# Local attention: the value projection and the output projection exchanged on TensorE, two reciprocal-root operations behind each mask operation

## The reference, cut to what matters

```
h = shift_token(x)
q, k, v = split(h @ wqkv, 3)                    # 8 heads of 64
q = q / max(norm(q), 1e-12) * qs                # the same for k, over each head
q, k = rotary_xpos(q, k)
sim = 8 * q @ k.T   over this window and the one before (128 + 128 keys)
attn = softmax(where(mask, -max, sim))
o = attn @ v
x = x + o @ wo
```

## Time and profile before

| | us |
|---|---|
| median of 3 runs | 2124.27 |
| lowest, highest | 2120.65, 2127.5 |
| the profiled execution, its own time | 2122.05 |
| its span, first to last instruction | 2120.3 |
| PE busy | 1900.5 (90%) |
| DVE busy | 1589.2 (75%) |
| ACT busy | 1098.0 (52%) |
| POOL busy | 449.2 (21%) |

### The profile page before, as it was taken

How to read it: one execution, slowest core, us unless ns; L and a number is a source line. 1 busy time by engine, 2 the same in 40 slices (tenths; PEclk the granted TensorE clock), 3 DMA queues, 4 the chain that set the end, 5 groups by cost and what they waited for, 6 DMA issues and landing times. The chain is left out here.

```text
span 2120.3 us, 41246 instructions
## 1 busy us (share of the span) xinstructions
PE 1900.5 (90%) x13304; PEld 1640.6 (77%) x13304; DVE 1589.2 (75%) x4668; ACT 1098.0 (52%) x2551; POOL 449.2 (21%) x270
## 2 busy tenths in 40 slices
PE   4678999899999759999999689995999999959998
PEld 4657888878889748888888578884888888858887
DVE  3367776776766668999999477775899999957777
ACT  2243343342342248888888434433777777743433
POOL 1130000000000024444444100002444444410110
PEclk7889999999999979999999799997999999989999
DMA  5410000000000020000000100001000000000002
GB/s 186 172 26 1 1 1 1 1 1 1 1 1 1 13 95 6 5 5 5 5 5 5 50 20 11 10 5 66 6 5 5 5 5 5 5 20 11 11 10 84
DMA packets 46083, 46.26 MB, mean 22 GB/s; under 512 B 8660, under 2 KB 40106, under 8 KB 45992
## 3 DMA queue, kind: packets, MB, share of 16 engines
q1 hardware_dynamic: 45992, 45.07, 6.4%
HBM read 36.67 MB, written 8.39 MB: 21 GB/s over the span
## 5 line engine op out<-in xcount | busy, mean ns | idle before, releaser
L993 ACT ACTIVATE l_probs<-l_probs,l_negmax 128x256 f32<-128x256 f32 x512 | 253.2, 496 | 64.7 <-DVE l_negmax L1074 64.7
L116 PE MATMUL ps<-local_w_hi,l_xT 128*128 128x512 f32 x384 | 166.9, 435 | 37.9 <-DVE l_xT L1067 31.9
L947 POOL TENSOR_TENSOR l_t<-l_t,l_t 128x1024 f32<-128x1024 f32 x64 | 152.8, 2388 | 195.8 <-DVE l_t L1120 195.8
L951 POOL TENSOR_TENSOR l_t<-l_t,l_rnorm 128x1024 f32<-128x1024 f32 x64 | 121.9, 1905 | 307.5 <-DVE l_rnorm L1091 307.5
L999 ACT ACTIVATE l_probsT<-ps 128x512 f32<-128x512 f32 x256 | 138.5, 594 | 53.4 <-PE ps L1218 53.4
L426 ACT ACTIVATE attn_exp<-ps 128x512 f32<-128x512 f32 x128 | 76.5, 599 | 152.1 <-PE ps L118 151.9
L118 PE MATMUL ps<-local_w_hi,l_xT 128*128 128x512 f32 x384 | 155.0, 404 | 0.0
L117 PE MATMUL ps<-local_w_lo,l_xT 128*128 128x512 f32 x384 | 154.7, 403 | 0.0
L116 PE MATMUL ps<-m_hnT_hi,ffn_w_hi 128*128 128x512 f32 (+1 forms) x352 | 142.8, 406 | 4.6 <-DVE m_hnT_lo L1457 4.6
L117 PE MATMUL ps<-m_hnT_lo,ffn_w_hi 128*128 128x512 f32 (+1 forms) x352 | 139.8, 397 | 0.0
L118 PE MATMUL ps<-m_hnT_hi,ffn_w_lo 128*128 128x512 f32 (+1 forms) x352 | 139.7, 397 | 0.0
(11 more groups left out here) (218 smaller groups left out, 5936.0 us busy)
## 6 DMA issues: line engine op xcount, KB each, us to landing
tok_x<-x SPq DMA_DIRECT2D x16, 512.0 KB, 9.6
m_shifted<-shifted SPq DMA_DIRECT2D x20, 256.0 KB, 2.8
shifted<-x SPq DMA_DIRECT2D x64, 64.0 KB, 1.5
out<-x SPq DMA_DIRECT2D x8, 512.0 KB, 4.5
ffn_w_raw<-ffn_w SPq DMA_DIRECT2D x6, 640.0 KB
local_w_raw<-ffn_wqkv SPq DMA_DIRECT2D x4, 768.0 KB, 5.2
tok_base<-attn_base SPq DMA_DIRECT2D x4, 512.0 KB
h<-txt SPq DMA_DIRECT2D x4, 512.0 KB, 11.9
```

Of the source, the lines that this page charges most:

```text
L116: nc.tensor.matmul(out, wh, mh, start=start, stop=False, skip_group_check=True)
L947: nc.gpsimd.tensor_tensor(t1[:], t1[:], t2[:], ALU.add).then_inc(s.summed.sem, 1)
L951: nc.gpsimd.tensor_tensor(r, r, rn[:].unsqueeze(2).to_broadcast([P, 2 * LH, DH]), ALU.mult).then_inc(s.rotated.sem, 1)
L993: last = nc.scalar.activation(v, v, ACT.Exp, bias=nb[:, h:h + 1], scale=-1.0, accum_out=rsum[:, h:h + 1])
```

## The change

Three orders of instructions are altered in `local_phase`; nothing is added or removed. On VectorE, the sum of squares now stands ahead of the addition to x, and `rnorm(3)` to `rnorm(10)` stand two behind each of the first four mask operations, so that the last four mask operations stand alone. On TensorE, the projection of v now follows the transposes of pairs 0 and 1, and the output projection follows those of pairs 2 and 3.

```
                 if a:
+                    nc.vector.tensor_reduce(ss[:], sq[:]..., AX.X, ALU.add).then_inc(s.sq_summed.sem, 1)
                 if d:
                     wait(dve, s.y_full, n - 2)
...
                     nc.vector.tensor_tensor(tile, ps[:, OT:OT + 1, 0:D], tile, ALU.add).then_inc(s.y_done.sem, 1)
                 if a:
-                    nc.vector.tensor_reduce(ss[:], sq[:]..., AX.X, ALU.add).then_inc(s.sq_summed.sem, 1)
                     wait(dve, s.sq_summed, n + 1)
...
+                k = 3
                 for h in range(LH):
                     if b:
...
                         score(n - 1, h, mask)
-                    if a:
-                        chain.wait()
-                        if 3 + h < LAST:
-                            chain.mark(rnorm(3 + h))
-                        else:
-                            rnorm(LAST).then_inc(s.rnorm.sem, 1)
+                    for _ in range(2):
+                        if a and k <= LAST:
+                            chain.wait()
+                            if k < LAST:
+                                chain.mark(rnorm(k))
+                            else:
+                                rnorm(LAST).then_inc(s.rnorm.sem, 1)
+                            k += 1
...
# TensorE
+                if b:
+                    wait(pe, s.v_done, n - 1)
+                    project(1 - r, 2, V).then_inc(s.v_full.sem, 1)
+                if c:
+                    for pair in (2, 3):
+                        wait(pe, s.p_done, 4 * (n - 2) + pair - 1)
+                        probs_t(n - 2, pair)
                 if d:
                     wait(pe, s.o_done, n - 2)
...
                     last.then_inc(s.y_full.sem, 1)
-                if c:
-                    for pair in (2, 3):
-                        wait(pe, s.p_done, 4 * (n - 2) + pair - 1)
-                        probs_t(n - 2, pair)
-                if b:
-                    wait(pe, s.v_done, n - 1)
-                    project(1 - r, 2, V).then_inc(s.v_full.sem, 1)
```

More of the change, by code:

```diff
@@ L1121, in step @@
                     last.then_inc(s.turned.sem, 1)
+                if a:
+                    nc.vector.tensor_reduce(ss[:], sq[:].rearrange("p a (h d) -> p (a h) d", d=DH), AX.X,
+                                            ALU.add).then_inc(s.sq_summed.sem, 1)
                 if d:
@@ L1128, in step @@
                 if a:
-                    nc.vector.tensor_reduce(ss[:], sq[:].rearrange("p a (h d) -> p (a h) d", d=DH), AX.X,
-                                            ALU.add).then_inc(s.sq_summed.sem, 1)
                     wait(dve, s.sq_summed, n + 1)
```

## The result

The changed kernel takes 2146.53 us (median of 4 runs, 2143.71 to 2150.65) beside 2123.84 for the one before: a ratio of 1.0095, with a 95% interval of 1.0079 to 1.011. That is slower by 22.7 us, against a forecast of 2154.6 and a range of 2128 to 2176. The profiled execution took 2143.71 us with a span of 2141.9, 21.6 us more than the span before.

A forecast was written before the change was run, and what follows sets the result against it. The prediction took VectorE's and ScalarE's mask-to-mask chain as the bound in B, with 0.24 us of slack in A. Growth of 0.68 and 0.44 us, 1.12 a pair over 29 pairs, added 32.5 to 2122.05: 2154.6 us, range 2128 to 2176.

The forecast's parts named there:

- What sets the interval: Local-phase loop: masks, exponentials, squares, rotation, L947, L1083 and the next mask set B, without TensorE or L951.
- A mask with two operations behind it: VectorE, masks 1 to 4: each takes 0.64 us to the next mask, making ScalarE's exponentials 0.68 us later.
- B: Loop interval with ScalarE's weight piece, 13.25 us between first masks; forecast to grow by the full 0.68 us.
- A: Loop interval without the weight piece, 13.20 us between first masks; 0.24 us of slack, forecast to grow by 0.44 us.
- 29 pairs: Count of interval pairs in the two layers' loops; each pair was to grow by 1.12 us, together 32.5 us.
- Fill and drain I leave out: Steps at the loop's edges: L951's earlier start gives back at most 1 us, later exponentials cost as much.
- The exchange costs nothing in the loop: TensorE in the loop: both projections take about 1.47 us, so x transposes, inverses and scores do not move.
- the addition behind the sum of squares: VectorE: the addition waits for `y_full` until 11.95 us; cost 0, since L947 covers it with 0.6 us left.
- The one that would have made the kernel faster: Rival: TensorE's 0.58 us wait for L951 was the pace and goes; at most 34 us gained, 2088; chance 0.07.
- The rival in which the second root operation hides: VectorE behind masks 1 to 4: a chained start as cheap as a free one, no change, 2125; chance 0.08.
- `y_full` did hold up the addition to x: Rival: late output projection holds up VectorE's chain, 11 us more, 2166; chance 0.10.
- The masks beside L951: Rival: masks 5 to 8 are held until L951 ends, costing 147 us, 2269; chance 0.03.

The follow-up runs named there:

- e5: The changed kernel with ScalarE's weight piece moved behind the copies of the transposed probabilities: 2135.6 us, ratio 1.0044 to the kernel before.
- e2: The kernel before with only the doubling, two root operations behind each of masks 1 to 4: 2153.38 us, ratio 1.0146.
- e1: The changed kernel with one root operation behind each mask again, both exchanges kept: 2119.06 us, ratio 0.9969.
- e6: The kernel before with only ScalarE's weight piece moved behind the copies of the transposed probabilities: 2125.14 us, ratio 0.9996.
- e9: The kernel before with TensorE's exchanged order only in the last three steps of each layer, 32 to 34: 2120.36 us, ratio 0.9974.
- e10: The kernel before with only the sum of squares put ahead of the addition to x: 2124.04 us, ratio 1.0004.
- e3: The kernel before with only TensorE's two projections exchanged, the addition to x still ahead of the sum of squares: 2177.88 us, ratio 1.0252.
- e7: The kernel before with rnorm(3) moved between the two operations of the low part of x, the others one behind each mask: 2113.72 us, ratio 0.9936.
- e8: The changed kernel's two exchanges without doubled root operations, with early rnorm(3) and the moved weight piece: 2101.54 us, ratio 0.9883 to the kernel before.

## Why the prediction was right, and where its sizes were off

*What sets the interval.* The chain from the masks through exponentials, squares, rotation, L947 and L1083 to the next mask was named as the one that bears the loss. e5 shows it for the changed kernel (0.35 us of ScalarE off, 0.35 us of the interval off), and e2 and e1 show that the doubling alone makes the loss of the loop.

*A mask with two operations behind it: 0.64 us.* Measured 0.64. The exponentials were to start at 1.10, 2.38 and 3.56 and end at 5.53; they start at 1.10, 2.38, 3.53 and end at 5.52. The squares were to be 0.68 later and are 0.67 later in B. Taken from rows of a stage in which the operations stand alone, the cost of a combination that no row showed came out within 0.01 us.

*"In B this is on the chain with nothing to hide it: +0.68. In A the 0.24 of slack takes a part: +0.44."* This is the term that was mis-sized. B grew by 0.60 and A by 0.35. The slack in the kernel before was 0.08 us larger in both than I had read. I took the missing idle time ahead of the mask at 1028.34 as proof that VectorE's own chain ended there. But L1067 starts at 1010.89 in the changed kernel and the mask follows 0.08 us later. In the kernel before these two rows stand:

```profile
1028.19 0.16 DVE L1067 TENSOR_SCALAR l_xT<-l_xT 128x2 fp32r<-128x2 f32 x1
1028.34 0.42 DVE L1074 CUSTOM_DVE_ANT_0 l_probs<-ps,l_mask_odd 128x256 f32<-128x256 f32 x1
```

0.15 us from one to the other: 0.07 of it was a wait, too short to be listed as idle, because the operation before was still running. e6 says the same: with VectorE's and ScalarE's chain 0.35 shorter in B, the interval stayed at 13.25. The scores say it too: the mask followed 1.19 us behind their start in both intervals of the kernel before (1013.90 to 1015.09, 1027.15 to 1028.34). So in the kernel before L951 and TensorE bounded both intervals, and the sentence that B's chain "does not pass through TensorE or L951 at all" was right only for the changed kernel. A pair grew by 0.95 us here (0.92 in the mean of the loop) and not by 1.12.

*29 pairs.* The loop from L951 of step 3 on has 28 intervals in a layer, so 28 pairs. 28 x 0.92 (767.2 - 741.4 = 25.8 us over 28 pairs) against 29 x 1.12: of the 6.7 us too much, 1 is the count and the rest the slack. The fill was not free: between the first masks of steps 1 and 3 it grew by 1.40 us in layer 0 and 0.34 in layer 1.

*"Fill and drain I leave out."* The drains gave back 4.8 us in the profiled execution, which was the other mis-sized term: it lay beyond the loop, and I had looked at TensorE's exchange only in the loop, where a projection of v covers the wait for the low part of o. e9 shows the gain alone, 3.7 us by the medians and 5.5 by the ratio. At one granted clock the order is worth about 2.6 of it, by the estimate above; the rest goes with the clock, which the prediction did not look at and which no run ties to the order.

*The exchange costs nothing in the loop, and the addition behind the sum of squares neither.* e1 and e10 show both. The two edits depend on each other: e3 has one without the other and loses 51 us, by the length that follows from reading L1083's 1.01 us as a hold. By the Trainium skill (SBUF — State Buffer, Who interferes with whom) such an instruction is blocked for as long as GpSimd holds the shared ports; the trace agrees, with 1.01, 0.62 and 0.17 us for the same instruction as it starts earlier or later beside L947.

*Rivals.* The one that would have made the kernel faster had a true part: L951 does bound the kernel before, and e7 gains by moving it. It fails for this change because the way chosen to get it earlier by 1.09 us delays the exponentials by 0.67 us. The rival in which the second root operation hides did not come: it starts 0.21 us behind the first. There the prediction gives the page's rule without its exception. The section (the Trainium skill, VectorE: DVE Perf Modes, The DRAIN you can't avoid) adds that a next operation that is not held starts earlier, and this trace agrees: the mask starts 0.09 us behind a root operation of 0.17. `y_full` did hold up the addition to x, by 0.42 us a step, but L1083 still waited for L947, and e1 has 0.75 us of that wait in a loop of the old length. The masks beside L951 were not held: masks 5 to 8 keep 0.35 us (1014.04 - 1013.69).

## What to carry to other kernels

Where one queue feeds two consumers, count what a new order does to both: this one gave one of them its input 1.09 us earlier and the other 0.67 us later, and the second was within 0.1 us of being the bound in one of two intervals. Shortening the path that was not the bound gained nothing (e6), shortening the other gained only until the first took over (e7, 6.4 us in the loop), and edits to both gained 16.7 us there (e8). A small operation added 0.21 us behind the one that it depends on and 0.09 us with an independent operation between them, so a chain is best threaded one at a time, and begun earlier if it has to end earlier (e7). A row without listed idle time does not say that nothing was waited for: compare its distance to the instruction before it with the same distance where no wait is possible.

## What the runs showed of the hardware

TensorE's granted clock in step 33 of layer 0 differed between executions of nearly the same work, and neither the order of the instructions nor the length of the wait ahead of them decided it alone. With the old order and a wait of 3.2 us it was 0.53 in the kernel before (1195 to 1205 us) and 1.00 in e10_sum_first_only (1196 to 1206 us). With the exchanged order and a wait of 2.72 us it was 1.00 in e1_one_behind (1195 to 1205 us) and 0.50 in e3_exchange_only (1224.3 to 1229 us). What did decide it stays open. The two drains together took 55.6 to 62.1 us in the profiled executions of the old order and 50.9 to 59.1 of the exchanged one, so a difference of a few us in such a stretch says nothing by itself; the granted clock has to be read beside it.

VectorE's L1083, a `tensor_scalar` of 128x16, took 1.01, 0.62 or 0.17 us, as it started 0.98 or 0.58 us ahead of the end of GpSimd's L947 or 1.2 us behind it.
